# Linear attention and mixture of experts on one core: tile 7 gets expert blocks of its own, its attention moves among them, and gathers add into the output rows

## The chip, the cores and the metric

The kernel runs on one core of one Trainium2 chip. The metric is the device time of one execution in microseconds (us). TensorE is called PE here, VectorE DVE, ScalarE ACT, GpSimd POOL, and SyncE, which issues the plain DMAs, SP. PEld is TensorE's weight load, and DVEq or SPq the instruction queue of an engine.

## The reference

Input x is (2, 2048, 256) in float32. One layer is computed:

```
xn  = layernorm(x)
q, k, v, u = xn @ W.T + b ; u, v = silu ; q, k = elu, 8 heads of 32
energy = (q k^T) * lower_triangle ; out = energy @ v      (no softmax)
attn = (u * rms_norm(out) * scale) @ Wo.T + bo
top1 = argmax(xn @ Wg.T)                                   (8 experts)
xhat = layernorm(xn)
ffn  = for each token, of its expert alone: gelu((xhat*s+b) @ W1 + b1) @ W2 + b2
y    = x + attn + ffn
```

Hidden size of an expert is 64. Since there is no softmax, attention over earlier tokens is a running 32x32 state per head.

## The kernel before, in words

There is no scheduler: each engine's program is written out by hand with semaphores. The 4096 tokens are cut into `TILES` = 8 tiles of 512 tokens (`CH` = 4 chunks of 128); even tiles belong to one batch row, odd ones to the other.

**Ticks.** `tick(i)` for i = 0 to 6 does, on every engine, the attention of tile i (scores, mask, `attend`, gate, product with Wo, added into the output rows `o[i]`) beside the projections of tile i+1 and the normalisation of tile i+2. On DVE a tick is, in order: elu of k, four masks, elu of q, four masks, `gated(i, 0)`, `norm_stats(i+2)`, router logits and choice of tile i+1, `gated(i, 1)`, states, counts, `mean_square`, `xnT_lo`, `reciprocal`, `add_attention`. POOL does small scalars (`norm_scalars`), sums and low halves, and the book-keeping of the experts, `book(n)`: from the counts it finds to which row of the scratch tensor `xs` each token goes; `scatter(n)` then sends the 512 normalised rows there with four indirect DMAs of 128 rows.

**Blocks.** In `xs` the tokens lie sorted by expert in blocks of 128 rows; an expert's last open block is filled further by the next tile. 39 blocks (`BLOCKS`, 32 full ones and 7 for the remainders) are run after the last tick. Per block: SP loads a pair of blocks (`load_pair`, 256 KB, four buffers), PE turns it (`turn_block`), ACT copies it out of PSUM (`features_block`), PE makes the hidden layer (`hidden_block`), ACT the gelu, PE the product (`product_block`), and DVE copies that to `y_blk`; `keep_pair` on SP writes pairs to `ys`. DVE also copies each block's expert weights out of `table` (`weights_block`) at an offset that it reads into a register (`load_experts`, `value_load` at L846). Copying weights takes DVE 0.36 us a block, ACT's two steps 0.38 and 0.36. PE's loop turns block k+4, makes hidden k+2 and product k.

**What sets the order around the change.** Since an open block may get rows of any later tile, no block can be loaded before the scatter of tile 7: `load_pair(0)` waits for all scatters. `expert_of_blocks` finds the experts of the first 24 blocks once, in tick 5; their 24 register loads stand in ticks 5 and 6, twelve each, just ahead of `gated(i, 1)`. `last_tick(7)` is the attention of tile 7 alone, ahead of the blocks. When enough pairs are in `ys`, POOL gathers the rows of tile n into `x_in` (`gather(n)`, four indirect DMAs), DVE adds them to `o[n]` (`add_experts`) and SP stores `o[n]`. After the last block come the gathers and stores of tiles that are left over.

In order listings below, `x4` at the end of a row counts instructions, `A<-B` is destination and sources.

## Time and profile before

| | us |
|---|---|
| median of 3 runs | 342.39 |
| lowest, highest | 341.08, 342.73 |
| the profiled execution, its own time | 343.99 |
| its span, first to last instruction | 342.2 |
| busy PE, PEld | 272.4, 231.8 |
| busy DVE, POOL, ACT | 206.7, 186.5, 158.7 |

All engines are read in microseconds from the start of the span. The page of a profile gives the busy share of each engine, a chain that leads back from the last instruction, and groups of instructions by line; the trace behind it answers for any stretch. A busy share says little here, because the kernel has three stages with different limits: ticks (to 247), the attention of the last tile and the wait for its scatter (to 264), and blocks with their gathers and stores (to the end). The mean granted clock of TensorE is 0.908 of its full 2.4 GHz.

### The profile page before, as it was taken

How to read it: one execution, taken by the hardware profiler on the slowest of the kernel's cores; microseconds unless marked ns; L12 is line 12 of the kernel's file. 1: busy time of each engine (PE TensorE's matmuls, PEld its weight loads, DVE VectorE, ACT ScalarE, POOL GpSimd, SP SyncE). 2: the span in 40 equal slices, each digit the busy share in tenths (PEclk: the TensorE clock that was granted, in tenths of full speed). 3: DMA queues.
4: the chain of work that ended last, by engine and by line, in shares of the span. 5: the costliest groups of instructions: out<-in, count | busy, mean ns of one | idle time of the engine just before them, and what ended most of it. 6: DMA issues, size and time to landing. Idle time of an engine off the chain costs nothing. (4 is left out here: it accounts for less than half of the span.)

```text
span 342.2 us, 7905 instructions
## 1 busy us (share of the span) xinstructions
PE 272.4 (80%) x2912; PEld 231.8 (68%) x2912; DVE 206.7 (60%) x530; ACT 158.7 (46%) x296; POOL 186.5 (54%) x414
## 2 busy tenths in 40 slices
PE   2598997999799799799979955995776999697600
PEld 2487785888679588687868945884756878576400
DVE  6787492695488179369648914781486355555621
ACT  2358256545834845664492536351221656444200
POOL 6336666575577567547657641762474002756671
PEclk9999899899899989989989995999698899989955
DMA  7997013004003201300402100110004466889985
GB/s 262 316 345 219 3 63 124 2 33 156 0 2 112 77 2 62 124 3 18 162 9 64 63 1 2 61 63 2 1 17 131 130 187 212 267 231 344 302 286 173
DMA packets 33510, 39.61 MB, mean 116 GB/s; under 512 B 2481, under 2 KB 30657, under 8 KB 33473
## 3 DMA queue, kind: packets, MB, share of 16 engines
q1 hardware_dynamic: 30176, 30.69, 27.6%
q0 software_dynamic: 3072, 8.39, 7.8%
q8 instruction: 23, 0.38, 0.5%
q14 instruction: 15, 0.11, 0.1%
q10 hardware_dynamic: 224, 0.03, 0.1%
HBM read 20.23 MB, written 18.87 MB: 114 GB/s over the span
## 5 line engine op out<-in xcount | busy, mean ns | idle before, releaser
L1161 POOL DMA_INDIRECT x_in<-ys,rows x32 | 32.6, 1018 | 41.5 <-DMA ys<-y_blk 32.0
L581 ACT ACTIVATE e_neg<-ring,cols 128x512 f32<-128x512 f32 x32 | 22.0, 689 | 50.1 <-PE ring L245 50.1
L243 PE MATMUL ring<-xn_hi,w_hi 128*128 128x512 f32 x96 | 41.1, 429 | 1.8 <-DVE xn_lo L727 1.7
L742 DVE TENSOR_TENSOR energy<-ring,causal 128x512 f32<-128x512 f32 x64 | 39.5, 682 | 0.1
L245 PE MATMUL ring<-xn_hi,w_lo 128*128 128x512 f32 x96 | 39.3, 409 | 0.0
L244 PE MATMUL ring<-xn_lo,w_hi 128*128 128x512 f32 x96 | 39.2, 409 | 0.0
L1150 POOL DMA_INDIRECT xs<-x_in,rows x32 | 32.8, 1026 | 11.6 <-issue 7.3
L766 DVE TENSOR_TENSOR g<-ring,uT 128x512 f32<-128x512 f32 x16 | 11.0, 687 | 37.3 <-ACT sq L598 20.3
L365 PE MATMUL ring<-xT_blk,w_blk 128*128 128x128 f32 x156 | 26.3, 294 | 4.5 <-DVE w_blk L855 4.1
L286 PE MATMUL kv_bank<-v_tok,k_tok 128*32 128x32 f32 x480 | 9.0, 228 | 26.0 <-ACT k_tok L594 25.3
L757 DVE TENSOR_TENSOR state<-state,kv_bank 128x256 f32<-128x256 f32 x30 | 12.6, 421 | 26.4 <-PE kv_bank L286 25.0
L872 DVE COPY y_blk<-ring 128x256 f32<-128x256 f32 x39 | 16.4, 423 | 19.9 <-PE ring L372 19.9
L286 PEld LDWEIGHTS kv_bank<-v_tok,k_tok 128*32 128x32 f32 x480 | 7.3, 139 | 30.1 <-issue 28.6
L365 PEld LDWEIGHTS ring<-xT_blk,w_blk 128*128 128x128 f32 x156 | 22.4, 206 | 7.0 <-issue 5.1
L623 ACT ACTIVATE xT_blk<-ring 128x256 f32<-128x256 f32 x39 | 14.9, 384 | 22.5 <-PE ring L356 22.4
L243 PEld LDWEIGHTS ring<-xn_hi,w_hi 128*128 128x128 f32 x96 | 18.7, 195 | 8.2 <-issue 3.9
L372 PE MATMUL ring<-w_blk,h_blk 128*128 128x256 f32 x78 | 23.9, 393 | 0.0
L1060 POOL TENSOR_TENSOR rms<-ms,half_pow 128x4 f32<-128x4 f32 x8 | 8.2, 1028 | 26.8 <-DVE ms L800 26.8
L1051 POOL TENSOR_TENSOR g_lo<-g,g_hi 128x512 fp32r<-128x512 f32 x14 | 17.6, 1269 | 9.6 <-ACT g_hi L618 9.6
L243 PE MATMUL ring<-wo_hi,g_hi 128*128 128x256 f32 x64 | 21.9, 342 | 0.6 <-DVE g_lo L865 0.6
L245 PEld LDWEIGHTS ring<-xn_hi,w_lo 128*128 128x128 f32 x96 | 18.9, 197 | 4.6
L244 PEld LDWEIGHTS ring<-xn_lo,w_hi 128*128 128x128 f32 x96 | 18.9, 197 | 3.6
(158 smaller groups left out, 759.7 us busy)
## 6 DMA issues: line engine op xcount, KB each, us to landing
xs<-blank SPq DMA_DIRECT2D x4, 1280.0 KB, 10.9
x_blk<-xs SPq DMA_DIRECT2D x20, 256.0 KB, 3.4
ys<-y_blk SPq DMA_DIRECT2D x20, 256.0 KB, 3.2
x_in<-in_x SPq DMA_DIRECT2D x8, 512.0 KB, 4.1
o<-in_x SPq DMA_DIRECT2D x8, 512.0 KB, 4.8
out<-o SPq DMA_DIRECT2D x8, 512.0 KB, 4.5
energy<-in_w_in SPq DMA_DIRECT2D x4, 256.0 KB, 4.5
energy<-in_w SPq DMA_DIRECT2D x1, 512.0 KB, 6.7
```

The lines of the kernel that those rows point to most:

```text
L243: pe.matmul(bk, w_h(k), x_h(k), start=(first and k == 0), stop=False, skip_group_check=skip)
L244: pe.matmul(bk, w_h(k), x_l(k), start=False, stop=False, skip_group_check=skip)
L245: ins_ = pe.matmul(bk, w_l(k), x_h(k), start=False, stop=(last and k == tiles - 1), skip_group_check=skip)
L286: last = pe.matmul(kv_part[c % 2][DH * m:DH * (m + 1), head], k_tok[:, c, head], v_tok[b][:, c, head], start=True, stop=True, skip_group_c ...
L365: last = pe.matmul(bk[:, KT * P:KT * P + P], w_blk[k % 4][:, t * HE:t * HE + P], xT_blk[k % 4][:, tok(t)], start=(t == 0), stop=(t == KT - 1))
L372: pe.matmul(bk[:, 0:D], h_blk[k % 3][:, :], w_blk[k % 4][:, W2_AT:HB_AT], start=True, stop=True).then_inc(s["y_pe"], 1)
L581: act.activation(e_neg[t][:, :], bk[:, :], ACT.Exp, bias=vecs[:, col:col + 1]).then_inc(s[f"{w}_exp"], 1)
L742: dve.tensor_tensor(energy[:, t, m, :].rearrange("p (c n) -> p c n", c=CH), bank(f"s{t}{m}", n)[:, :].rearrange("p (c x) -> p c x", c=CH), ...
L872: dve.tensor_copy(y_blk[j][:, k % 2, :], block_bank(k)[:, 0:D]).then_inc(s["y"], 1)
L1051: pool.tensor_tensor(g_lo[:, t, :], g[:, t, :], f32(g_hi[:, t, :]), ALU.subtract).then_inc(s["g_lo"], 1)
L1150: pool.indirect_dma_start(out=xs, out_offset=bass.IndirectOffsetOnAxis(ap=rows[:, n, c:c + 1], axis=0), in_=x_in[n % 3][:, c, :], in_offse ...
L1161: pool.indirect_dma_start(out=x_in[n % 3][:, c, :], out_offset=None, in_=ys[0:blocks * P, :], in_offset=bass.IndirectOffsetOnAxis(ap=rows[ ...
```

## The change

1. **Blocks of its own for tile 7.** Tiles 0 to 6 (`CLOSED` = 7) share blocks as before; after tile 6 POOL sets `fill` back, so that tile 7 opens new blocks. There are 28 + 7 + 4 + 7 = 46 blocks (23 pairs) instead of 39. `load_pair(0)` waits for the scatters of tiles 5 and 6 alone, `load_pair(14)` for that of tile 7.
2. **Tile 7's attention among the last blocks.** After tick 6 PE makes the scores of tile 7 and DVE its eight masks; then the blocks begin. `attend` for the two halves stands after blocks 35 and 38, the square sums after block 42, in the bank `kv_bank`; the product with Wo after the last block.
3. **Statistics first.** `norm_stats(i+2)` is the first step of DVE's tick, and POOL's `norm_scalars` for it stands between `book` and `scatter` of the tick before.
4. **Experts of the blocks, tile by tile.** `find_experts(i)` (five small instructions) in every tick, and four register loads per tick: two ahead of `gated(i, 1)` and two ahead of `reciprocal(i)`. Tile 7's is done after block 5, and the 18 loads of blocks 28 to 45 every second block after it.
5. **ACT takes every third product** (k = 2, 5, 8, ...) out of PSUM, DVE the others.
6. **Gathers that add.** `gather(n)` writes to `o[n]` with `compute_op=ALU.add`. `add_experts` and its semaphore are gone; SP's stores wait for the gather itself and stand a little later. For tile 7 the gather adds to the residual and DVE adds the attention after it.

The core of the diff:

```diff
+CLOSED = TILES - 1
+BLOCKS = CH * CLOSED + NE - 1 + CH * (TILES - CLOSED) + NE - 1
+PAIRS = BLOCKS // 2
+LATE = CH * CLOSED + NE - 1
-BACK = CH + NE - 1 + 9
+BACK = CH + NE - 1 + 11
...
+        def product_of(k):
+            return (s["y_act"], k // 3 + 1) if k % 3 == 2 else (s["y_dve"], k - (k + 1) // 3 + 1)
...
+            def load_expert(k, n):
+                dve.wait_ge(s["expert"], n + 1)
+                weights_at[k] = dve.value_load(expert[k:k + 1, 0:1], min_val=0, max_val=(NE - 1) * WROW)
...
+                if norm_next:
+                    norm_stats(m)
                 elu(n, "k", 0, bank("k0", i))
...
-                if i >= TILES - 3:
-                    j = (i - (TILES - 3)) * EARLY // 2
-                    load_experts(j, j + EARLY // 2)
+                find_experts(i)
+                load_expert(CH * i, i)
+                load_expert(CH * i + 1, i)
                 gated(i, 1, bank("att1", i))
...
-            last_tick(TILES - 1)
+            i = TILES - 1
+            mask(i, 0)
+            mask(i, 1)
...
+            dve.wait_ge(back_sem[i % 3], 64 * (i // 3 + 1))
+            add_attention(i, 0, block_bank(BLOCKS))
+            add_attention(i, 1, block_bank(BLOCKS + 1))
...
+                pool.wait_ge(*((s["added"], 2 * (n + 1)) if n < TILES - 1 else (res[n % 2], 16 * (n // 2 + 1))))
...
-                    pool.indirect_dma_start(out=x_in[n % 3][:, c, :], out_offset=None, in_=ys[0:blocks * P, :],
-                                            in_offset=bass.IndirectOffsetOnAxis(ap=rows[:, n, c:c + 1], axis=0)
-                                            ).then_inc(back_sem[n % 3], 16)
+                    pool.indirect_dma_start(out=o[n][:, c, :], out_offset=None, in_=ys[0:blocks * P, :],
+                                            in_offset=bass.IndirectOffsetOnAxis(ap=rows[:, n, c:c + 1], axis=0),
+                                            compute_op=ALU.add).then_inc(back_sem[n % 3], 16)
...
-                    for b in (0, 1):
-                        sp.wait_ge(scattered[b], 64 * (TILES // 2))
+                    for n in (CLOSED - 2, CLOSED - 1):
+                        sp.wait_ge(scattered[n % 2], 64 * (n // 2 + 1))
+                if pair == CH * CLOSED // 2:
+                    n = TILES - 1
+                    sp.wait_ge(scattered[n % 2], 64 * (n // 2 + 1))
```

On DVE, in tick 0, between the last mask and the states (`g` is the gate, `onehot` the choice, `expert` the table offsets). Before:

```order
L766 TENSOR_TENSOR g<-ring5,uT0 128x512
L709 BN_STATS stats<-x_in2 128x6 x4
L715 BN_AGGR mv<-stats 128x2 x4
L771 COPY logit<-ring6 128x8
...
L789 TENSOR_TENSOR onehot<-hit,win 128x32
L766 TENSOR_TENSOR g<-ring3,uT0 128x512
```

The same place now:

```order
L785 TENSOR_TENSOR g<-ring5,uT0 128x512
L790 COPY logit<-ring6 128x8
...
L808 TENSOR_TENSOR onehot<-hit,win 128x32
L848 TENSOR_SCALAR past<-first_block,block_col 128x8
...
L857 CAST expert<-expert_f 128x1
L862 TENSOR_LOAD expert
L862 ISA x2
L785 TENSOR_TENSOR g<-ring3,uT0 128x512
```

The statistics have left this place for the head of the tick, and five instructions and two register loads stand ahead of the second gate in every tick.

On PE, after tick 6: first the scores of tile 7 (L300), then, before:

```order
L300 MATMUL ring<-qT,kT 128x128 x32
L312 MATMUL ring<-qT,state_11 128x128
L312 MATMUL ring<-qT,state_1 128x128 x3
L317 MATMUL ring<-energy,v_tok 32x128 x16
...
L326 MATMUL ring<-ident,sq 128x128 x4
...
L356 MATMUL ring<-ident,x_blk 128x128 x6
L365 MATMUL ring<-xT_blk,w_blk 128x128 x2
```

and now:

```order
L310 MATMUL ring<-qT,kT 128x128 x32
L366 MATMUL ring<-ident,x_blk 128x128 x6
L375 MATMUL ring<-xT_blk,w_blk 128x128 x2
L366 MATMUL ring<-ident,x_blk 128x128 x2
L375 MATMUL ring<-xT_blk,w_blk 128x128 x2
```

The first block is turned right behind the scores; attend, square sums and the product with Wo have left this place.

## Rows read from the trace of the kernel before

**Rows 1.** Stretches of all engines: length, busy, PEclk, DMA share, GB/s

```profile
172.70:174.80 2.10, 0.00 (x0) 0.00 (x0) 0.27 (x1) 1.86 (x5) 2.10 (x3) 1.00 0.00 0
177.00:179.80 2.80, 2.80 (x24) 2.74 (x16) 2.44 (x6) 2.79 (x5) 0.75 (x1) 0.50 0.00 0
...
288.70:322.40 33.70, 27.36 (x169) 22.30 (x168) 20.08 (x47) 14.96 (x41) 22.78 (x22) 0.95 0.89 277
...
310.00:316.00 6.00, 5.30 (x39) 4.67 (x39) 3.82 (x9) 3.45 (x10) 3.54 (x5) 1.00 1.01 333
```

**Rows 2.** ACT in order of time: start, us, instruction, idle before and releaser

```profile
154.15 0.69 ACT L581 ACTIVATE e_neg<-ring,cols 128x512 f32<-128x512 f32 x1 [2.54 <-PE ring L245]
...
169.63 2.08 ACT L604 ACTIVATE xn<-x_in,shift,rstd 128x256 f32<-128x256 f32 x4 [2.27 <-POOL shift L1038]
...
182.85 0.69 ACT L581 ACTIVATE e_neg<-ring,cols 128x512 f32<-128x512 f32 x1 [2.94 <-PE ring L245]
...
217.42 0.69 ACT L581 ACTIVATE e_neg<-ring,cols 128x512 f32<-128x512 f32 x1 [2.87 <-PE ring L245]
```

**Rows 3.** DVE in order of time, ticks 4 to 6 and the masks of tile 7

```profile
165.01 1.40 DVE L709 BATCH_NORM_STATS2 stats<-x_in 128x6 f32<-128x256 f32 x4
166.45 0.38 DVE L715 BATCH_NORM_AGGREGATE mv<-stats 128x2 f32<-128x6 f32 x4
...
172.28 0.69 DVE L766 TENSOR_TENSOR g<-ring,uT 128x512 f32<-128x512 f32 x1 [4.06 <-ACT sq L598]
...
183.57 0.48 DVE L733 TENSOR_SCALAR e_neg<-e_neg 128x512 f32<-128x512 f32 x1 [1.23 <-ACT e_neg L581]
...
206.26 0.69 DVE L766 TENSOR_TENSOR g<-ring,uT 128x512 f32<-128x512 f32 x1 [8.20 <-issue]
...
231.24 0.19 DVE L789 TENSOR_TENSOR onehot<-hit,win 128x32 bf16<-128x32 f32 x1
238.81 0.69 DVE L766 TENSOR_TENSOR g<-ring,uT 128x512 f32<-128x512 f32 x1 [7.38 <-issue]
...
248.34 4.88 DVE L742 TENSOR_TENSOR energy<-ring,causal 128x512 f32<-128x512 f32 x8
```

**Rows 4.** DVE's register loads: duration ns min/median/max, first and last start

```profile
L846 DVEq TENSOR_LOAD <-expert x39: 302/313/766, 198.1 to 282.8; - x39
```

**Rows 5.** PE in order of time: scores of tick 5, then the last stage and blocks

```profile
188.24 1.17 PE L300 MATMUL ring<-qT,kT 32*128 32x128 f32 x32
...
247.15 1.67 PE L300 MATMUL ring<-qT,kT 32*128 32x128 f32 x38
...
251.25 1.08 PE L317 MATMUL ring<-energy,v_tok 128*32 128x128 f32 x32
252.26 1.16 PE L312 MATMUL ring<-qT,state 128*128 128x128 f32 x8
...
265.50 1.06 PE L365 MATMUL ring<-xT_blk,w_blk 128*128 128x128 f32 x4
...
268.78 0.60 PE L372 MATMUL ring<-w_blk,h_blk 128*128 128x256 f32 x2
...
285.96 0.60 PE L372 MATMUL ring<-w_blk,h_blk 128*128 128x256 f32 x2
...
287.06 0.60 PE L372 MATMUL ring<-w_blk,h_blk 128*128 128x256 f32 x2
...
320.85 1.46 PE L372 MATMUL ring<-w_blk,h_blk 128*128 128x256 f32 x6
```

**Rows 6.** The page's groups: busy us, mean ns of one, idle before and releaser

```profile
L872 DVE COPY y_blk<-ring 128x256 f32<-128x256 f32 x39 | 16.4, 423 | 19.9 <-PE ring L372 19.9
```

**Rows 7.** POOL's first gather of tile 7, in order of time

```profile
330.48 0.98 POOL L1161 DMA_INDIRECT x_in<-ys,rows  x1 [0.31 <-issue]
```

**Rows 8.** The end of the chain that ended last

```profile
323.80 3.88 DMA ys<-y_blk
...
334.31 3.24 DMA x_in<-ys,rows
```

202 lines of the change are left out of this document (101 added, 101 removed).

## The prediction

> **What bounds the kernel now.** I read the profile in three views: the engines in order of time for the tick lengths, then the same for the way from the last tick to the first block, then busy stretches for the blocks.
>
> A regular tick takes 28.7 us: ACT's first exponential of tick 4 starts at 154.15, that of tick 5 at 182.85 [rows 2]. PE is the busiest engine in it, but it stands still once, for 2.1 us at 172.7, and in the stretch at 177.0 its granted clock is 0.50, that is the 1.2 GHz level [rows 1]. The stop comes from a chain: statistics on DVE, their roots on POOL, and ACT waiting 2.27 us for the shift before it can normalise the next tile [rows 2], square att1 and release DVE's second gate (idle 4.06 us before it, [rows 3]).
>
> Ticks 5 and 6 are longer. From 182.85 to 217.42 tick 5 takes 34.57 us [rows 2]; DVE does not compute for 8.20 us before its second gate there, and for 7.38 us in tick 6, from 231.43 to 238.81 [rows 3]. That is where the 24 register loads stand [rows 4]: 7.38 / 12 = 0.62 us each.
>
> Then comes the hole: PE makes the scores of tile 7 at 247.15, and the first hidden layer of a block starts at 265.50 [rows 5]. The blocks wait for the scatter of tile 7; its attention is done in the meantime.
>
> Blocks run from 268.78 (first product) to 322.3 (end of the last) [rows 5]. Undisturbed, a block takes 287.06 - 285.96 = 1.10 us, limited by PE [rows 5]. From 288.7 to 322.4, with gathers and stores, the DMA engines are 0.89 busy and move 277 GB/s; 333 GB/s is what they move when full [rows 1]. From 322.3 to 342.2, 19.9 us, only the tail is left.
>
> **The change part by part.** The sum is made in the span of 342.2 us. The profiled execution took 343.99 as a whole, 1.8 more; the median of the runs, 342.39, is 0.2 above the span, and that 0.2 is added at the end.
>
> *Ticks 5 and 6.* Each now has 4 loads instead of 12, and `find_experts` of five small operations. The trace shows the same five in tick 5 alone: idle 8.20 less twelve loads of 0.62 leaves 0.8 us outside the loads, so a plain step costs about 1.2 us with its own run time. Tick 5 becomes a regular tick with the surcharge worked out below: 34.57 - 28.7 - 0.4 = 5.5 us less. In tick 6, which normalises nothing, the second gate moves from 238.81 to 231.43 + 1.2 + 2 x 0.62 = 233.9, so 4.9 us less; its other two loads fit into DVE's wait for POOL's root. **Together -10.4.**
>
> *Ticks 0 to 4.* Here nothing was wrong with loads, so they now pay for them: 4 x 0.62 + 1.2 = 3.7 us more work on DVE. Against that, DVE idles 4.06 us before the second gate and 1.23 us at the head of the tick [rows 3], 5.3 together. Statistics first takes ACT's 2.27 us wait away. But what is late next is DVE itself. It ends the tick 1.2 us later (two loads ahead of `reciprocal`), then does the statistics, 1.40 + 0.38 = 1.8 us [rows 3], where only 1.23 us of idling is there: elu and masks come 1.8 us later or a little more. PE, which began the second scores right when the third mask let it (188.24, 6.98 us into its tick, [rows 5]), waits about 2 us there, and so values, logits and choice come some 2 us later. With 1.2 us for the experts and 1.2 us for two loads the second gate lands 0.4 us later than now. So the 2.1 us stop of PE is traded for one of 2 us earlier in the tick. Without the stop at 172.7 the low clock at 177.0 may go, worth half of about 3.2 us at 0.50, 1.6 us; behind the new stop it may come back. I take +0.2 for each, **+1.0 for five**, with -1.6 and +2.0 per tick as bounds.
>
> POOL's five scalars move ahead of `scatter`, 2.5 us in every tick to 4; DVE has the statistics ready by the time the rows are booked, and the scatter's rows are wanted only a tick later. I cost it at nothing; it would cost its 2.5 us once if a load of x came late. The 7 more blocks also make `xs` longer to blank, 0.9 MB more at the start while POOL and PE set up; nothing on the path, at most 2.5 us.
>
> Tick 6 then ends at 247.15 - 10.4 + 1.0 = **237.8**.
>
> *The hole.* DVE finishes adding tile 6 1.2 us after that, then does eight masks, 4.88 us [rows 3], then the first weights, 0.36. PE can turn blocks meanwhile, as far as masks free its banks. So hidden layer 0 starts 6.4 us after tick 6; from there to the first product it took 268.78 - 265.50 = 3.3 us [rows 5]. First product: 237.8 + 9.7 = **247.5**, against 268.78: 21.3 us earlier, of which 9.4 are the ticks'. The scatter of tile 7 is covered: it is wanted by pair 14, loaded after block 19, 21 us behind the first product; it lands some 14 us after tick 6.
>
> *Blocks.* Until gathers start DVE held them back by one load per block: from 268.78 to 285.96 thirteen took 1.32 us each [rows 5]. Now there is a load every second block and DVE copies two products of three, 0.42 us each [rows 6]: 0.36 (weights) + 0.28 + 0.31 = 0.95 us, under PE's 1.10. ACT has 0.38 + 0.36 + about 0.4 for every third product, below PE too; I take its share at nothing (bounds 0 to 2 us over the phase, were it to hold up a turn). Gather 0 needs 6 pairs, so blocks 0 to 11: 11 x 1.10 + 0.5 for `find_experts` = 12.6, to **260.1**.
>
> *From block 12 on* PE wants 34 x 1.10 = 37.4 us, and for the attention inside the loop 2 x (1.16 + 1.08) [rows 5] + 0.6 for the square sums = 5.1, together 42.5. The DMA engines have 17 pairs in and out, 17 x 0.524 = 8.9 MB (a pair is 256 KB each way), 7 gathers, 3.7 MB, and 4 stores, 2.1 MB: 14.7 MB. At 277 to 333 GB/s [rows 1] that is 44 to 53 us; at 300, 49. So the DMA engines set this stage, and the seven blocks of tile 7 are paid in transfers more than in PE. Last product ends at 260.1 + 49.5 = **309.6**.
>
> *What an adding gather costs* no row shows. The rows bound it: a plain gather at one end, for which the 3.7 MB are in the sum already (and 1.2 us of DVE per tile go, which is below nothing for DVE but off PE's path); at the other end two and a half times the transfer time, if each 1 KB row needs a read of its own in SBUF and a slower pass. Taken: a quarter more, 3.7 MB / 4 / 300 GB/s = **3 us**, near the plain end, because the bytes from HBM and the packets stay the same and part of the extra falls where the DMA engines have room, behind block 35. The Trainium skill (Collectives: The Full Stack, "The bandwidth ceiling: the fold count and why AG ≠ RS ≠ AR") says that the add itself is free but that it needs two source reads on the same ring, which halves the rate. No run here shows it yet; by it the sum would be 12 us, not 3.
>
> *The tail* is 19.9 us now. Its chain is: product, DVE's copy, 3.88 us to `ys`, four gathers at 1.26 us, 3.24 us for the last [rows 8], the add, the store. Gather 7 began at 330.48 though its data had landed at 323.80 + 3.88 = 327.68, because POOL was still issuing that of tile 6 [rows 7, 8]. Between the needs of gathers 6 and 7 now lie 11 blocks instead of 4, so 2.6 us go. The copy came 0.9 us late behind an add of DVE, which goes. The last add is four 256-column steps, 1.66 against 1.23 us: +0.4. **Tail 16.8.**
>
> Sum: 309.6 + 3 + 16.8 = 329.4 for the span, **329.5** for the time.
>
> **The rivals.** *Doubled gathers.* If an add costs twice a copy on the DMA engines, 3.7 MB / 0.3 = 12.2 us instead of 3: 338.7. For it: the DMA engines are the bound of this stage in my own sum. Against it: POOL issues a gather only every 5 us, so it fills holes.
>
> *Short ticks.* If DVE keeps up, PE's stops shrink below a microsecond and its clock stays at 2.4 GHz, six ticks lose 1.6 us each, 9.6: 320. For it: 5.3 us of idle DVE against 3.7 us of new work. Against it: the masks.
>
> *Long ticks.* Both stops in a tick, each followed by a stretch at 1.2 GHz: +2 for six ticks, 341.
>
> *Slower than before.* Adding gathers hold the DMA queues, `load_pair` comes late, and SP, which waits for the gather itself before each store, has the next load queued behind that wait. From a cost of 2.3 times a plain gather on, (342.2 - 326.4) / 12.2 = 1.3 over one, the whole gain is eaten. At two and a half times it is 345.
>
> *The change does not do what it says:* early blocks wait after all, for a scatter or weights, so that the first product comes 8 us later: 337. The waits named in the code speak against it.
>
> **How the numbers follow.** Chances: 329.5 (325 to 334) 0.42, doubled gathers 0.22, short ticks 0.16, long ticks 0.09, slower 0.08, late first block 0.03. Within 0.5% of 342.4 (which a measurement of this kernel can't tell from no change) lie 1.7 us to each side, 340.7 to 344.1: parts of the doubled-gather and long-tick cases, 0.05. Slower by over 0.5% 0.08, faster 0.87. The range leaves out the slower case and the outer part of short ticks: 320 to 341.
>
> **What would show it.** Right: ticks of about 29 us all alike, DVE's idle before the second gate near 1.5 us; PE's first product near 248; 46 products, the last near 310 to 312; DMA share near 0.9 or more from 261 on, PE's turns waiting for `x_blk`; the last gather starting as soon as the last pair has landed; a tail near 17. Wrong: packet time of the gathers' queue doubled at equal bytes (doubled gathers); granted clock at 1.00 in the whole tick (short ticks); SP waiting for gathers with loads behind. My weakest steps are the adding gather and the trade of stops in a tick.

## The result and the profile after

The changed kernel takes **316.48 us**, median of runs from 316.16 to 319.16, beside 341.74 for the kernel before: ratio 0.9285, 95% interval 0.9217 to 0.9352. Its profiled execution took 316.16 with a span of 314.4. An execution now and then falls into a slower state of the chip: the medians here are of all executions, the ratios leave those out. Forecast were 329.5, with a range of 320 to 341. The direction was right, the gain (25.3 us) was twice the one forecast (12.9), and the time lies 3.5 us below the range. The traced execution of the kernel before took 343.99 us, more than its medians, so that the two traces lie 27.8 us apart.

From here on "tick" is counted at ACT's first exponential, as in the prediction. After, in order of time (start, us, engine, line and operation, idle before it and its releaser); these answer to [rows 2]:

```profile
143.51 0.69 ACT L588 ACTIVATE e_neg<-ring,cols 128x512 f32<-128x512 f32 x1 [1.88 <-PE ring L255]
...
157.32 2.06 ACT L611 ACTIVATE xn<-x_in,shift,rstd 128x256 f32<-128x256 f32 x4
...
170.16 0.69 ACT L588 ACTIVATE e_neg<-ring,cols 128x512 f32<-128x512 f32 x1 [1.87 <-PE ring L255]
```

Tick 4 now takes 170.16 - 143.51 = 26.65 us (before 28.70), and `xn` no longer waits for POOL. All ticks are like that: the starts are 37.26, 63.57, 90.18, 116.82, 143.51, 170.16 and 196.31, where before had 37.03, 67.23, 96.18, 125.17, 154.15, 182.85 and 217.42.

DVE around the start of tick 4, which answers to [rows 3]:

```profile
140.41 1.28 DVE L746 TENSOR_TENSOR xn_lo<-ring,xn_hi 128x512 fp32r<-128x512 f32 x2
141.94 0.18 DVE L823 RECIPROCAL rinv<-rms 128x4 f32<-128x4 f32 x1 [0.26 <-POOL rms L1076]
142.16 1.66 DVE L831 SCALAR_TENSOR_TENSOR o<-ring,rinv,o 128x256 f32<-128x256 f32 x4
143.73 1.40 DVE L728 BATCH_NORM_STATS2 stats<-x_in 128x6 f32<-128x256 f32 x4
...
147.69 2.47 DVE L761 TENSOR_TENSOR energy<-ring,causal 128x512 f32<-128x512 f32 x4
```

Two register loads stand between `xn_lo` and `reciprocal`, and yet `reciprocal` starts 0.26 us after `xn_lo`. At the same place before, without any load, it was this:

```profile
180.39 0.18 DVE L804 RECIPROCAL rinv<-rms 128x4 f32<-128x4 f32 x1 [0.23 <-POOL rms L1062]
```

PE, which answers to [rows 5]: second scores and the stop in tick 4, then the scores of tile 7, the first hidden layer, the first and the last product:

```profile
148.90 1.87 PE L310 MATMUL ring<-qT,kT 32*128 32x128 f32 x32
...
163.22 0.46 PE L296 MATMUL kv_bank<-v_tok,k_tok 128*32 128x32 f32 x32 [0.53 <-ACT k_tok L601]
...
220.14 1.43 PE L310 MATMUL ring<-qT,kT 32*128 32x128 f32 x36
...
227.01 0.68 PE L375 MATMUL ring<-xT_blk,w_blk 128*128 128x128 f32 x4 [2.31 <-DVE w_blk L870]
...
228.86 0.60 PE L382 MATMUL ring<-w_blk,h_blk 128*128 128x256 f32 x2
...
291.79 1.46 PE L382 MATMUL ring<-w_blk,h_blk 128*128 128x256 f32 x6
```

Stretches (from and to, length, busy time of PE, PEld, DVE, ACT, POOL, then PEclk, DMA share, GB/s), which answer to [rows 1]:

```profile
162.00:164.00 2.00, 1.47 (x43) 1.22 (x42) 0.26 (x1) 2.00 (x5) 1.70 (x2) 1.00 0.88 303
170.00:172.00 2.00, 2.00 (x25) 1.46 (x26) 1.97 (x9) 1.14 (x2) 1.50 (x7) 1.00 0.17 29
...
228.80:241.60 12.80, 12.46 (x91) 10.83 (x90) 7.25 (x23) 9.11 (x26) 2.89 (x3) 1.00 0.68 208
241.60:276.10 34.50, 28.90 (x197) 23.94 (x196) 15.24 (x41) 20.87 (x58) 25.52 (x17) 1.00 1.00 260
276.10:293.20 17.10, 14.54 (x150) 12.36 (x150) 8.47 (x20) 8.42 (x23) 14.35 (x10) 1.00 0.98 231
```

PE's stop at the turn of a tick was this in the trace of before (in [rows 1] it is the stretch with nothing on PE):

```profile
174.84 0.46 PE L286 MATMUL kv_bank<-v_tok,k_tok 128*32 128x32 f32 x32 [2.21 <-ACT k_tok L594]
```

It is down from 2.21 us to 0.53, and the granted clock behind it is 1.00, the 2.4 GHz level; before it was 0.50, 1.2 GHz [rows 1]. All regular ticks are alike in this.

Gathers, from the page (DMA queue: packets, MB, share of 16 engines' span; then GpSimd's group: count, busy us, mean ns, idle before):

```profile
q0 software_dynamic: 6144, 8.39, 12.7%
...
L1176 POOL DMA_INDIRECT o<-ys,rows x32 | 50.2, 1568 | 23.0 <-DMA ys<-y_blk 14.2
```

The page of before has for the same queue:

```profile
q0 software_dynamic: 3072, 8.39, 7.8%
```

And POOL at the end, which answers to [rows 7]: the last gather of tile 6, the root for tile 7's attention, and the first and last gather of tile 7; under it the end of the chain, which answers to [rows 8]:

```profile
296.27 1.54 POOL L1176 DMA_INDIRECT o<-ys,rows  x1 [0.30 <-issue]
297.26 1.63 POOL L1074 TENSOR_TENSOR rms<-ms,half_pow 128x4 f32<-128x4 f32 x1
...
299.82 1.63 POOL L1176 DMA_INDIRECT o<-ys,rows  x1 [0.64 <-issue]
...
305.49 1.55 POOL L1176 DMA_INDIRECT o<-ys,rows  x1 [0.30 <-issue]
```

```profile
303.64 1.55 POOL o L1176
305.49 3.81 DMA o<-ys,rows
```

Where the 27.8 us between the two traced executions lie, by the way from one mark to the next:

| stretch | before | forecast | after | after less forecast |
|---|---|---|---|---|
| start of tile 7's scores | 247.15 | 237.8 | 220.14 | -17.7 |
| from there to the first product | 21.6 | 9.7 | 8.7 | -1.0 |
| first product to the end of the last | 53.5 | 65.1 | 64.4 | -0.7 |
| the tail behind it | 19.9 | 16.8 | 21.15 | +4.35 |
| span | 342.2 | 329.4 | 314.4 | -15.0 |

So the blocks came out as forecast. The ticks were wrong by nearly 18 us, and the tail by 4 the other way.

### The profile page after: what moved, and what is told of

Read it like the earlier page. It is cut to its first block and busy times, and to the rows that moved or that the text cites. A ratio compares the mean times of both kernels' runs of the same rounds, so it can differ in the third digit from the quotient of the medians.

```text
span 314.4 us, 8159 instructions
## 1 busy us (share of the span) xinstructions
PE 267.0 (85%) x2968; PEld 226.5 (72%) x2968; DVE 201.9 (64%) x551; ACT 167.7 (53%) x325; POOL 205.8 (65%) x409
## 3 DMA queue, kind: packets, MB, share of 16 engines
q0 software_dynamic: 6144, 8.39, 12.7%
## 5 line engine op out<-in xcount | busy, mean ns | idle before, releaser
L1176 POOL DMA_INDIRECT o<-ys,rows x32 | 50.2, 1568 | 23.0 <-DMA ys<-y_blk 14.2
L1164 POOL DMA_INDIRECT xs<-x_in,rows x32 | 32.3, 1009 | 11.5 <-issue 10.4
L375 PE MATMUL ring<-xT_blk,w_blk 128*128 128x128 f32 x184 | 28.6, 278 | 4.9 <-DVE w_blk L870 4.9
L630 ACT ACTIVATE xT_blk<-ring 128x256 f32<-128x256 f32 x46 | 17.4, 381 | 24.2 <-PE ring L366 24.1
L382 PE MATMUL ring<-w_blk,h_blk 128*128 128x256 f32 x92 | 27.1, 380 | 0.0
L887 DVE COPY y_blk<-ring 128x256 f32<-128x256 f32 x31 | 13.1, 421 | 21.4 <-PE ring L382 21.4
L870 DVE COPY w_blk<-table 128x385 f32 x46 | 17.2, 384 | 12.5 <-PE ring L382 10.7
L310 PEld LDWEIGHTS ring<-qT,kT 32*128 32x128 f32 x512 | 18.3, 186 | 7.5 <-issue 5.1
L310 PE MATMUL ring<-qT,kT 32*128 32x128 f32 x512 | 22.5, 286 | 1.0 <-DVE o L831 0.3
L366 PE MATMUL ring<-ident,x_blk 128*128 128x128 f32 x92 | 17.9, 278 | 6.0 <-DMA x_blk<-xs 5.9
L366 PEld LDWEIGHTS ring<-ident,x_blk 128*128 128x128 f32 x92 | 11.7, 141 | 13.2 <-issue 9.9
```

What stands on the lines that cost most here:

```text
L310: last = pe.matmul(bank(f"s{t}{m}", n)[:, tok(c)], kT[b][rows, t, tok(c)], qT[b][rows, t, tok(c)], start=True, stop=True, tile_position=(D ...
L366: last = pe.transpose(bk[:, tok(t)], x_blk[j][:, k % 2, tok(t)], ident[:, :])
L375: last = pe.matmul(bk[:, KT * P:KT * P + P], w_blk[k % 4][:, t * HE:t * HE + P], xT_blk[k % 4][:, tok(t)], start=(t == 0), stop=(t == KT - 1))
L382: pe.matmul(bk[:, 0:D], h_blk[k % 3][:, :], w_blk[k % 4][:, W2_AT:HB_AT], start=True, stop=True).then_inc(s["y_pe"], 1)
L630: act.activation(xT_blk[k % 4][:, :], block_bank(k)[:, 0:KT * P], ACT.Copy).then_inc(s["features"], 1)
L1164: pool.indirect_dma_start(out=xs, out_offset=bass.IndirectOffsetOnAxis(ap=rows[:, n, c:c + 1], axis=0), in_=x_in[n % 3][:, c, :], in_offse ...
```

## The experiments

Theory A is what the two traces suggest: *statistics first* is worth 2 to 3 us in every tick since the loads that were to spoil it cost nothing; the blocks of tile 7's own and its late attention shorten the 20 us hole; the adding gathers cost time in the tail only. Theory B differs from run to run and stands in the expectations.

All times are medians with the kernel before run beside them. That kernel took 339.0 us beside the first four runs below, and 362.4 to 364.9 beside all the others, so that only ratios and neighbours can be compared. "Elsewhere" stands below for these slower surroundings. The changed kernel was run again there three times (below, "The changed kernel elsewhere"), but not on the chip of four of the runs: the wait for the scatter of tile 7, the attention among the first blocks, the root behind the gathers, and the first run with the filled stop. These are set against its three ratios. The expectations put the two levels down to different chips. The record doesn't bear that out: chip number 14 stands beside the 339.0 and also beside 364.9, so why the level changed is open.

### Statistics late

The changed kernel with the statistics and POOL's scalars where they were before:

```diff
-                norm_next = m < TILES
-                if norm_next:
-                    norm_stats(m)
+                norm_next = m < TILES
                 elu(n, "k", 0, bank("k0", i))
...
                 gated(i, 0, bank("att0", i))
+                if norm_next:
+                    norm_stats(m)
```

and on POOL `norm_scalars(m)` behind `scatter`, ahead of `squares`, as before.

> The changed kernel with one part undone: statistics back behind the first gate on DVE, and POOL's scalars back behind scatter. Theory A (the regular ticks became 2.3 us shorter because statistics first takes PE's stop of 2.1 us away and the clock no longer falls behind it): six ticks go back from 26.6 to about 28.8 us, with a stretch at 0.50 in each, time about 316.5 + 13 = 329. Rival B (the tick gain has another source, as experts found tile by tile or transfers that moved): ticks stay near 26.6, time within 2 us of 316.5.

Measured 329.03 us, ratio 0.9699 (0.9622 to 0.9777), as theory A had it. This one edit is worth 12.5 us by the times (against 316.48) and 14 by the ratios (against 0.9285). Ticks 0 to 5 start at 37.66, 66.48, 94.36, 123.33, 152.30 and 181.26, so a regular one is 28.96 us long, 2.3 more than in the changed kernel, and the stop of the kernel before is back in each. The low clock is back too, except in one tick, the one from 66.48 to 94.36. PE at the stop, a stretch within it, and then that tick and the next one, each up to the end of its stop and from there on:

```profile
173.23 0.46 PE L296 MATMUL kv_bank<-v_tok,k_tok 128*32 128x32 f32 x32 [2.36 <-ACT k_tok L601]
```

```profile
171.00:173.20 2.20, 0.00 (x0) 0.00 (x0) 0.36 (x1) 1.96 (x5) 2.20 (x3) 1.00 0.00 0
...
66.48:87.40 20.92, 18.58 (x214) 15.42 (x213) 14.90 (x41) 11.64 (x21) 14.47 (x36) 1.00 0.23 77
87.40:94.36 6.96, 6.79 (x111) 6.10 (x112) 5.30 (x14) 4.81 (x9) 3.70 (x9) 1.00 0.01 2
94.36:115.30 20.94, 18.59 (x214) 15.44 (x213) 14.92 (x41) 11.66 (x21) 14.47 (x36) 1.00 0.23 76
115.30:123.33 8.03, 8.03 (x111) 7.31 (x112) 5.58 (x14) 4.79 (x8) 4.12 (x12) 0.79 0.01 3
```

The two ticks are the same kernel in the same execution, alike up to the end of the stop. Behind it PE runs the same matmuls (111 records), in 6.96 us at a granted clock of 1.00 and in 8.03 at a mean of 0.79. So the low clock costs 1.1 us a tick, and it does not follow on every stop of this length. The tick without it is 27.88 us long, so that the other 1.2 us over the changed kernel's 26.65 are the stop, less what statistics first costs elsewhere in the tick.

### Statistics first, and nothing else

The other way round: the kernel before with only that move (and POOL's scalars, likewise ahead of `scatter`).

> The kernel before with statistics first alone. Theory A: ticks 0 to 4 fall from 28.9 to about 26.6 us; tick 5 gains little, because its twelve loads still hold the second gate; the rest as before: 342 - 12 = 330. Rival B: ticks stay near 28.9, time within 2 us of 342. Theory of the prediction (masks come later and cost what the gate gains): 342 too, with a new stop of 2 us at the second scores.

Measured 330.19 us, 0.9745 (0.9675 to 0.9815): a gain of 8.85 us of 339.04, 6 to 11 by the interval, so theory A and neither rival. Its regular ticks are 26.17 us long (115.89, 142.05, 168.22) and the 2.2 us stop of PE at their turn is gone. That is 0.5 us less than in the changed kernel: what five operations of `find_experts` and four register loads cost a tick. Ticks 5 and 6 still hold the twelve loads each (35.09 us for tick 5). By itself the move gives 8.85 us; taken away from the changed kernel it costs 12.5 to 14. By the traces, tick 6 starts 14.1 us sooner than in the kernel before (203.31 against 217.42), and the span ends 13.9 us sooner (328.3 against 342.2), so what the ticks gain reaches the end. That this is 5 us more than the medians say lies in the traced execution of the kernel before: it took 343.99 us, where the median beside this run is 339.04. Where those 5 us lie in it, no trace shows.

### Loads twice

Four loads ahead of `reciprocal` instead of two, to price the step that the forecast leaned on:

```diff
                 load_expert(CH * i + 2, i)
                 load_expert(CH * i + 3, i)
+                load_expert(CH * i + 2, i)
+                load_expert(CH * i + 3, i)
                 reciprocal(i)
```

> The changed kernel with the two register loads ahead of the reciprocal made twice in each tick, four instead of two. Theory A (DVE's queue makes these loads while the low half of xn is still being computed, 1.28 us, so the two cost nothing): four take 2.5 us against 1.5 us of cover, so DVE ends each tick 1 us later and elu and masks with it: between 0 and 1 us per tick, 317 to 323. Rival B (a load costs its 0.62 us wherever it stands, as the prediction had it): 1.24 us per tick of seven, 325, and the reciprocal 1.24 us later.

Measured 324.95 us, 0.9601 (0.9533 to 0.9669), 8.5 us over the changed kernel's 316.48 and nearly 11 by the ratios. `reciprocal` now idles 1.20 us instead of 0.26:

```profile
143.72 1.28 DVE L746 TENSOR_TENSOR xn_lo<-ring,xn_hi 128x512 fp32r<-128x512 f32 x2
146.19 0.18 DVE L823 RECIPROCAL rinv<-rms 128x4 f32<-128x4 f32 x1 [1.20 <-POOL rms L1078]
```

The trace has the four loads from 143.7 to 146.1, so they start with `xn_lo` and run beside it, and `reciprocal` follows at their end. In the changed kernel the two are there from 140.3 to 141.5, while `xn_lo` computes until 141.69. Four loads of 0.62 us are 2.5; `xn_lo` and POOL's root cover 1.28 + 0.26 = 1.5 of them, and the 0.95 left is what appears. Two loads, 1.24 us, fit under the cover: their price is nothing. The regular tick is 27.6 us long, 1.0 more than in the changed kernel, so past the cover every microsecond counts in full. The time as a whole is the 325 of B (which has no cover) and outside A's 317 to 323, though the tick and the 0.95 are A's: the ticks make up only about 5.3 of the 8.5 us. From the second half of tile 7's scores to the first product it is 9.8 us instead of 7.0, and from 234 to 236 PE's granted clock is 0.50 there, where the changed kernel has 1.00. The cover is shown by the tick, not by the total.

### Plain gathers

The changed kernel with gathers into `x_in` and the addition on DVE, as before:

```diff
-                for c in range(CH):
-                    pool.indirect_dma_start(out=o[n][:, c, :], ..., compute_op=ALU.add)
+                for c in range(CH):
+                    pool.indirect_dma_start(out=x_in[n % 3][:, c, :], ...)
...
+                if k >= 22 and (k - 22) % CH == 0:
+                    add_experts((k - 22) // CH)
```

> The changed kernel with gathers that only copy into x_in and eight adds on DVE, as before. Theory A (an adding gather has twice the packets, takes 1.54 instead of 0.96 us of POOL, so that POOL falls behind and the last gather starts late): POOL issues at 1.26 instead of 1.85 us, the last gather starts as its pair lands, the tail falls from 21 to about 17.5 us, and PE's waits for blocks (5.9 us in all) shrink: 308 to 313. Rival B (taking 1.22 us adds off DVE between blocks was worth more than that): 318 to 321.

Measured 310.16 us, 0.9154 (0.9089 to 0.9219), in A's range, and the lowest time of all. That is 6.3 us below the changed kernel by the times and 4.5 by the ratios, whose intervals just touch; the traces below put it at 5.9. Its page, the same queue from 245 on (to 308.6), where only gathers are in it, its stretch from 241.6 on, and POOL at the end:

```profile
q0 software_dynamic: 3072, 8.39, 8.5%
...
L1186 POOL DMA_INDIRECT x_in<-ys,rows x32 | 32.9, 1029 | 29.4 <-DMA ys<-y_blk 16.6
...
q0 software_dynamic: 1536, 4.20, 23.0%
```

```profile
241.60:276.10 34.50, 29.99 (x203) 24.54 (x202) 18.36 (x44) 21.52 (x59) 21.45 (x21) 1.00 0.89 273
```

```profile
297.34 1.06 POOL L1186 DMA_INDIRECT x_in<-ys,rows  x1 [2.00 <-issue]
...
301.24 0.95 POOL L1186 DMA_INDIRECT x_in<-ys,rows  x1 [0.30 <-issue]
```

The last product ends at 293.34, in the changed kernel at 293.25: the block stage is equally long with plain and with adding gathers, although the queue's packet time is 26.2 us of 16 engines here (8.5% of 308.6) and 39.9 there (12.7% of 314.4). The engines have the room: from 276.1 to 293.2 their share is 0.74 here and 0.98 there. All of the difference is behind it, 15.3 us against 21.15. In its four steps: last product to the first gather of tile 7, 4.0 against 6.6; from the first to the last gather, 3.90 against 5.67; its landing up to the add, 2.79 against 3.89; the add, 1.23 against 1.66. That is 2.6 + 1.8 + 1.1 + 0.4 = 5.9. The first of these goes with the stores to `ys`: that of the last pair takes 2.3 us from issue to landing here and 4.5 in the changed kernel.

### The changed kernel elsewhere

Beside a kernel before that takes over 360 us, the changed kernel itself, three times:

> The changed kernel itself, beside the next ones on one chip, since chips differ (the kernel before took 339 us on one and 363 on another): 0.92 to 0.935 of the kernel before.

Measured 326.98 us, 0.9025 (0.8916 to 0.9134), with the kernel before at 362.71. The ratio is below the 0.92 to 0.935 that were expected.

> The changed kernel itself once more, to have it beside the three that follow in this list. Ticks of 26.6 us on a chip whose TensorE has no stops without a releaser, some 27.9 us on one that has them; span 314 or 324 us accordingly; and from the last product to the end 21 to 23 us in both cases.

Measured 328.18 us, 0.9001 (0.894 to 0.9063), at 364.88. The span is 325.3, about the 324 expected for such surroundings; the time behind the last product is 20.5 us, a little under the 21 to 23 expected.

> The changed kernel once more, beside the run with plain gathers that follows. Where the kernel before takes 339 to 342 us on the chip: 316 us. Where it takes 360 to 365 us: 327 us.

Measured 328.15 us, 0.9087 (0.9008 to 0.9166), at 362.35, as expected. So here the change takes 35 to 37 us off instead of 25, and the changed kernel is 11 us slower than in its first profile. PE shows short stops that no semaphore explains, in the midst of a run of matmuls that wait for nothing; this is one in a tick of the last of these three:

```profile
161.69 0.85 PE L327 MATMUL ring<-energy,v_tok 128*32 128x128 f32 x23
162.85 0.49 PE L327 MATMUL ring<-energy,v_tok 128*32 128x128 f32 x9 [0.31 <-issue]
```

The first profile of this kernel has none there. Ticks are some 27 to 29 us long instead of 26.6, with some of that behind such stops and some in a longer wait for `k_tok` (1.22 us). What these surroundings do to the chip the profile does not say.

### Statistics late, elsewhere, with and without its stop filled

To part the stop from the clock: the statistics-late kernel again, and the same with 16 matmuls of 256 columns that nobody reads in PE's stop, which keep PE at work until ACT's `k_tok` comes.

> Statistics late again (e1_stats_late), as the base for the next one on the same chip: 12 to 14 us more than the changed kernel.

> The changed kernel with statistics late (ticks of 28.9 us, 329.0 as a whole), and 16 matmuls of 256 columns on constant weights in PE's stop ahead of the states, results thrown away. Theory A (of the 2.3 us per tick that statistics first gave, some 1.6 us were the stop itself and the rest the low clock behind it): the stop stays, the granted clock stays at 1.00, ticks shorten by 1.0 to 1.6 us: 320 to 323. Rival B (the clock was not the cause, or the filling is paid in full): 329 or more.

> Statistics late and PE's stop filled with 16 matmuls again, now beside its base. In e10_clock_filled the granted clock stayed at 1.00, but PE had 2.6 us of stops of its own in each tick on that chip. Theory A (half of the tick gain is the low clock behind the stop): 1.0 to 1.6 us less per tick than the base, 6 to 10 us in all. Rival B: within 2 us of the base or slower.

Measured 346.27 us, 0.9535 (0.943 to 0.964), without the filling, 19.3 over the changed kernel where 12 to 14 were expected; with it 341.88, 0.9384 (0.9288 to 0.9479), on a chip where neither of the other two ran, and beside the first 341.87, 0.9433 (0.9347 to 0.9519). With it the granted clock is at 1.00 throughout the regular ticks; this is from the run on the chip of its own:

```profile
177.00:180.00 3.00, 2.62 (x21) 2.35 (x20) 0.69 (x1) 2.76 (x6) 2.17 (x2) 1.00 0.00 0
180.00:183.00 3.00, 2.59 (x84) 2.36 (x85) 1.36 (x4) 2.73 (x5) 1.59 (x2) 1.00 0.02 5
183.00:186.00 3.00, 2.85 (x24) 2.63 (x23) 2.60 (x8) 2.46 (x5) 1.40 (x3) 1.00 0.00 0
```

Beside its base the filling gains 4.4 us by the medians and 3.7 by the ratios, less than A's 6 to 10, more than B's 2, and the intervals of the two ratios overlap: by the times it is not settled. The ticks say more. The filled kernel's from tick 1 to 4 are 30.0 to 30.1 us long. Those of its base (traced in an execution of 348.67 us), where the clock falls to 0.50 behind the stop, are 31.2 to 31.3; the base has one, from 131.40 to 161.46, in which the clock stays at 1.00, and that one is 30.06 us long, the same as with the filling. So the filling is free in the tick and what it saves is the clock, 1.2 us wherever it would fall, and this agrees with the 1.1 of the statistics-late kernel above. Of the 2.3 us that statistics late adds to a tick, the clock is about one half and the stop the other.

### Pair 0 waits for the scatter of tile 7

```diff
-                    for n in (CLOSED - 2, CLOSED - 1):
+                    for n in (CLOSED - 1, CLOSED):
                         sp.wait_ge(scattered[n % 2], 64 * (n // 2 + 1))
```

> The changed kernel with load_pair(0) waiting for the scatters of tiles 6 and 7 instead of 5 and 6, so that no block is loaded before tile 7 is scattered, as before. Theory A (what the early start gives is the hole, and it is not given back later, since the block stage has a length of its own): the first product comes at about 243 instead of 228.9, time 316.5 + 13 = 329 to 331. Rival B (the DMA engines and POOL's gathers set the end, and blocks that start later catch up since they are no longer starved): 319 to 324.

Measured 338.49 us, 0.934 (0.928 to 0.94): 11.5 us over the first of the changed kernel's runs elsewhere, and 9 to 12 by its three ratios: near the 13 of theory A, and not the 3 to 7 of B. Beside the trace of that run the first product starts at 251.92 instead of 238.78 and the last one at 313.69 instead of 301.90. PE's waits from 215 on (line, releaser: total us, times, longest):

```profile
PE ring L366 <- DMA x_blk<-xs: 16.4, 9, 11.9
```

So the blocks of tile 7's own, which let pair 0 be loaded without its scatter, are worth some 12 us (13.1 at the first product), nearly all of which reaches the end.

### Tile 7's attention among the first blocks

```diff
-        LATE = CH * CLOSED + NE - 1
+        LATE = 0
```

> The changed kernel with the attention of tile 7 among blocks 0 to 8 instead of 35 to 43. Theory A (the stage from block 12 on is set by transfers and POOL's issues, and late attention lies in their shadow): the first blocks, which PE limits, pay its 5 to 6 us, the later stage does not give it back: 319 to 322. Rival B (PE sets the whole block stage, so its work costs the same wherever it stands): 315.5 to 317.5. Rival C (the engines for transfers gain room by blocks that start later and attention that is gone from the end): 312 to 315.

Measured 333.17 us, 0.9186 (0.912 to 0.9252), 6.2 us over the first of the changed kernel's runs elsewhere and 3.6 to 6.7 by its three ratios. Theory A expected 2.5 to 5.5 more, so it is the nearest; B (1 us at most) and C (less time) fit worse, though the intervals of the ratios touch. Moving the attention costs about as much as its own work (5.1 us by the prediction). That among the late blocks it fills time in which PE would wait is the reading that fits; the traced execution of this run is one of 337.94 us and was not set against another for it.

### The root behind the last gathers

```diff
-            root(TILES - 1)
             gather(TILES - 1)
+            root(TILES - 1)
```

> The changed kernel with POOL's root of tile 7 behind the last gather instead of ahead of it. Theory A (POOL issues gathers without a pause from 245.7 to 297.8 and then needs 2.0 us for the root, so its queue starts the last gather late): the last gather starts 2.0 us earlier, the root hides under its landing: 314 to 315. Rival B (the last pair lands only at the same time): 316 to 317.

Measured 325.70 us, 0.9011 (0.8932 to 0.9089), where the changed kernel took 326.98 (0.9025) on another chip: not to be told apart. The trace says why:

```profile
309.44 1.54 POOL L1176 DMA_INDIRECT o<-ys,rows  x1 [1.78 <-issue]
```

POOL stands idle for 1.78 us ahead of the first gather of tile 7, where with the root in between it was 2.02 us from gather to gather. The gather comes 6.9 us after the last product's end, in the changed kernel there 6.6. So the root is worth 0.2 us at most on the path, which is rival B; something else, nearly as late, releases the gather, and the last rows' landing in `ys` is what it waits for in the code.

### Plain gathers again

> The changed kernel with plain gathers (x_in as target, DVE adds, as in the kernel before). Theory A (what the adding gathers cost is GpSimd's issue time, 1.54 us each where a plain one takes 0.96, so that they run behind through the block stage and the last tile's four start late): 4 to 7 us less than the changed kernel in this list, all of it behind the last product. Theory B (the first such run, 6 us below the changed kernel on different chips, was the difference of the chips): within 1.5 us of it.

> The changed kernel with plain gathers and DVE adds, for a third time. Theory A (the shorter tail is worth 5 to 6 us, and what took it away in the second such run were stops of TensorE without a releaser in the block stage, 1 to 2 us each, that this chip has and the first had not): on a chip where the kernel before takes about 340 us, 309 to 311 us, so 5 to 7 less than the changed kernel beside it; on one where it takes about 363 us, within 3 us of the changed kernel on either side, with its tail some 4 us shorter and its block stage that much longer. Theory B (the plain gathers are worth nothing anywhere): within 1.5 us of the changed kernel on either chip and with a tail of the same length.

> Plain gathers as in the run above, and in GpSimd's queue the root of tile 7's gate norm comes behind the last tile's four gathers instead of ahead of them. Theory A (with plain gathers GpSimd is no longer behind, so the last four gathers wait for the last rows to be written and a root of 1.3 us ahead of them is hidden in that wait): no less than the run above, within 1 us; and if the root is waited for by the last attention rows' reciprocal, up to 1.5 us more. Theory B (the root stands on the path to the last gathers, as in the changed kernel, where this move gave 1.3 us): 1 to 2 us less than the run above.

Measured 329.87 us, 0.9016 (0.8945 to 0.9087), where the changed kernel took 328.18; 329.02 us, 0.907 (0.8997 to 0.9142), where it took 328.15; and with the root behind the gathers 330.59 us, 0.9059 (0.8967 to 0.9151). None differs from the changed kernel by more than is uncertain. That is not the 4 to 7 us of the first theory A; the second one, which asked for a shorter tail and a longer block stage in these surroundings, holds in the direction. Moving the root gives nothing here, as its theory A had it. The last of the three shows where the gain went. (The other two were traced in executions of 332.77 and 335.72 us; their tails are 15.1 and 14.9 us, their block stages 76.8 and 80.7.) Its tail is 17.05 us (309.35 to 326.4), that of the changed kernel beside it 20.5 (304.77 to 325.3): the 3.5 us are there. But its block stage is 70.2 us long against 65.6. PE's waits from 240 to 320 in it:

```profile
PE ring L375 <- issue: 3.6, 5, 1.3
PE ring L366 <- DMA x_blk<-xs: 2.8, 2, 2.0
```

The 3.6 us are five stops without a releaser; the changed kernel beside it has none of them on this line. So plain gathers shorten the tail in either surroundings. In the one run without such stops they won 4.5 to 6 us; in the three with them they won nothing. Why plain gathers bring more of them isn't shown.

### Half of the gathers adding

Adding gathers for tiles 0 to 3, plain ones for tiles 4 to 7 whose additions DVE makes behind the last blocks.

> The changed kernel with adding gathers for tiles 0 to 3 and plain ones with a DVE add for tiles 4 to 7. Theory A (the doubled packets cost through POOL's backlog and the tail alone): POOL is free again before the last pair lands, and DVE makes four adds fewer among the blocks than with plain gathers only: 5 to 8 us less than the changed kernel. Rival B (it matters where the transfer engines are full, in the early part): half the gain of plain gathers, 3 us.

> Adding gathers for tiles 0 to 3 and plain ones for tiles 4 to 7, the same kernel as the run with half of them adding. Theory A (the stop of 9.5 us on TensorE in the block stage, without any releaser, belongs to this kernel: its queues): it comes again, 8 to 11 us more than the changed kernel. Theory B (the stop belonged to that chip or that profile): no such stop, and a time between the changed kernel's and the plain gathers', so 2 to 5 us less than the changed kernel.

Measured 336.75 us, 0.9288 (0.9203 to 0.9373), and 337.14, 0.9204 (0.9117 to 0.929): 9 to 10 us over the changed kernel beside it both times, which no theory had in the first run; the second was to tell whether the chip or the kernel did it, and since it came again on another chip (9.0 us, in A's 8 to 11) it goes with the kernel, in these surroundings. The block stage stands still, at the same place in both. From the second, PE, ACT and DVE:

```profile
289.73 0.44 PE L367 MATMUL ring<-ident,x_blk 128*128 128x128 f32 x2
...
296.69 0.38 ACT L631 ACTIVATE xT_blk<-ring 128x256 f32<-128x256 f32 x1 [8.37 <-remote]
...
298.17 0.42 DVE L888 COPY y_blk<-ring 128x256 f32<-128x256 f32 x1 [9.59 <-remote]
299.56 1.19 PE L376 MATMUL ring<-xT_blk,w_blk 128*128 128x128 f32 x4 [6.93 <-DVE w_blk L871]
```

ACT's `xT_blk` waits by the code for PE's transposes of its block (which ended at 290.2) and for a hidden layer three blocks back, both done by 291.8, and it starts 5 us later than that. DVE stops at a copy that waits for a store of `y_blk` too. It falls where POOL issues twelve plain gathers in a row without a pause, right behind sixteen adding ones. Several engines stopped at once with their inputs there would fit engines that don't get their instructions; that is argued and not shown. Full DMA engines do not explain it all: in the second run their share is 1.1 until 292 and 0.4 from 296 on, with the computing engines still mostly idle. The cause stays open.

## Why the prediction was wrong

**Ticks 0 to 4: the step that failed.** Forecast +0.2 us each, measured 26.6 instead of 28.9 us (and 26.3 instead of 30.2 for tick 0): 132.9 us for the five instead of 145.8, so 13.9 of the 15 us that the span was off. The step had three faults.

- *"It ends the tick 1.2 us later (two loads ahead of `reciprocal`)."* It does not: `reciprocal` starts 0.26 us behind `xn_lo` with the loads and 0.23 without. The loads were priced from a place where DVE had nothing to compute, 0.62 us each, and laid end to end with arithmetic. Here they run while `xn_lo` does (140.3 to 141.5), and POOL's root was awaited there anyway. Four of them do show, by 0.95.
- *"Elu and masks come 1.8 us later or a little more", PE "waits about 2 us there".* The masks begin 4.18 us into the tick (147.69) instead of 3.25, 0.93 later, and the second scores begin at the same 5.39 us and take 1.87 instead of 1.17 us [rows 5]: 0.70 for PE. A stop of 2.2 us was traded for 0.53 and 0.70, not for one of 2. Two readings behind this were off: 188.24 is 5.39 us into the tick as the prediction counts it, from 182.85 (the 6.98 count from 181.26, PE's own start), and no mask held PE there: in the trace of before it goes into the second scores without idle time.
- *The clock.* The text had it right that the low clock might go without the stop, but let it come back behind the new stop, which never was. It put the clock at 1.6 us; it is 1.1. Tick 4 is 2.05 us shorter, of which the stops and scores are 2.21 - 0.53 - 0.70 = 0.98, and the 1.07 left agrees with the pair of ticks in the statistics-late kernel (8.03 - 6.96).

The prediction had this case as its rival "short ticks", at 0.16, and gave for it 320 us. It took 1.6 us off the forecast of each of six ticks, where 2.8 were needed, and it weighed "5.3 us of idle DVE against 3.7 us of new work" on its side less than the masks. The sum of the idle and the new work was the better guide. The kernel before with the statistics first shows it from the other side: everything that DVE got on top costs 0.5 us a tick.

**Ticks 5 and 6.** Forecast -5.5 and -4.9. Tick 5 is 26.15 us, 8.4 less, 2.9 more than forecast, again the regular tick being short. Tick 6, from 196.31 to 220.14 instead of from 217.42 to 247.15, is 5.9 us less, 1.0 more than forecast.

**The hole.** First product 8.7 us behind the start of tile 7's scores, forecast 9.7. Eight masks and the first weights follow as foreseen, and the first hidden layer starts at 227.01, 6.9 us behind the scores, forecast 6.4. From there to the first product it is 1.85 us where 3.3 were copied from the trace of before: a hidden layer took 1.06 us there [rows 5] and takes 0.68 now, at a granted clock of 1.00 from 227 to 229. That pair 0 does not wait for tile 7's scatter is worth some 12 us by itself, as its run showed, and this was the right reading of the change.

**The blocks.** Forecast 65.1 us with the gathers' 3, measured 64.4. DMA share 1.00 and 0.98, PE waiting for `x_blk` 5.9 us in eight pieces, and the late attention costing less there than among the first blocks: as written. But that the sum came out is in part luck: the 3 us for adding are not in there. With plain gathers the stage has the same length at a share of 0.89 and 273 GB/s, so that the DMA engines alone do not set it.

**The adding gather.** The prediction took 3 us, because "the bytes from HBM and the packets stay the same", and set against "doubled gathers" that "POOL issues a gather only every 5 us". Only the bytes stay. From 245 us on the queue has gathers only, and this is it in the changed kernel (to 314.4):

```profile
q0 software_dynamic: 4608, 4.20, 40.5%
```

That is 144 packets for a gather instead of 48, at equal bytes (the run with half of them adding fits, with 4608 on its page), and 28.1 us of packet time on 16 engines (40.5% of 69.4) against 14.6 with plain gathers (23.0% of 63.6): 1.9 times. By the rule of the Trainium skill (Collectives: The Full Stack, "The bandwidth ceiling: the fold count and why AG ≠ RS ≠ AR") that the add is free but wants two source reads and so halves the rate, the trace agrees in the time: 28.1 against 14.6 us. And POOL issues a gather every 1.85 us, not every 5. Of the 13.5 us more, 11.8 belong to the 28 gathers of tiles 0 to 6, which the rival "doubled gathers" put at 12.2. So it had the mechanism and the amount right. What it had wrong is that they lie on the path: the block stage is as long with plain gathers.

**The tail: the other failed step.** 21.15 us instead of 16.8. The text priced the adding gather in transfer time alone and let gather 7 start as soon as its data are there. What it does not have is GpSimd: it takes 1.54 us to issue an adding gather and 0.95 for a plain one ([rows 7] has 0.98), one every 1.85 us against 1.26. That is 1.8 us on the last four, and POOL, which issues gathers without a pause from 245.70 to 297.8, still keeps the queues full when the last rows are to be stored: the last pair takes 4.5 us to land in `ys`, with plain gathers 2.3. So the first gather of tile 7 starts 6.6 us behind the last product instead of 4.7 (330.48 - 322.31 less the 2.6 and 0.9 that were to go). The last one's landing takes 3.81 us instead of 3.24. Together 1.9 + 1.8 + 0.6 = 4.3. That the full queues are what makes the stores slow is a reading, not shown by a run of its own; it agrees with both pairs (6.6 and 6.9 with adding gathers, 4.0 and 4.4 with plain ones), and the run with the root moved leaves at most 0.2 us for the root.

**The side of the sign.** "Slower than before" needed the adding gathers to stall the loads. The loads did take longer, 4.7 us from issue to landing in the median against 3.4 before, but 4.4 of it with plain gathers too, and PE waits 5.9 us for `x_blk` with adding gathers and 4.6 without: nothing like the 12 us that the case needed.

**The base of the sum.** The sum was made in the span of an execution that took 343.99 us, and 0.2 us were added for the time. Both traced executions take 1.8 us more than their span, so a forecast from that trace was 331.2; this is small against the rest.

## What to carry to other kernels

Price an operation that is added to a queue where it will stand, not where it stood: register loads that took 0.62 us each in an idle stretch took nothing under a running instruction, and only what sticks out beyond the cover is paid. When a chain crosses three engines, count idle time of the engine that gets the work against the work; if it fits, take the short case as the likeliest. When a stop and a low clock come together, look for a tick of the same kernel that has the one without the other: it parts them better than two medians do. And before handing an addition to a DMA, look at the queue that issues it: the packet time of the gathers nearly doubled and cost nothing in the block stage, while the issue time of the last four and the slower landings around them stood at the end.

## What the runs showed of the hardware that was not expected

- A DVE register load (about 0.31 us, 0.62 in a row of them) goes on while the instruction ahead of it still computes: two under a 1.28 us `xn_lo` cost 0, four 0.95 us.
- An adding indirect gather of 128 rows of 1 KB has 144 packets where a plain one has 48, 1.9 times its packet time at equal bytes, and GpSimd needs 1.54 us instead of 0.95 to issue it.
- A stop of 2.35 us on PE was followed by a stretch at 0.50 in most ticks and not in all. With it the rest of the tick took 8.03 us, without it 6.96. With 16 matmuls that nobody reads in the stop, the clock stayed at 1.00 in all regular ticks.
- The same kernel takes 316 us beside a kernel before of 342, and 327 to 328 beside one of 362 to 365, with stops of PE that have no releaser; one chip number stands at both levels. A variant won 4.5 to 6 us in the one and nothing in the other: compare only side by side.
- Twelve plain gathers issued without a pause behind sixteen adding ones come with a stop of all computing engines of 7 to 13 us, twice at the same place, whose cause is open.
